# A graph layer whose table is multiplied first: W*W1 formed once, one product behind each pair of tiles, six banks for the sums

## The chip, the cores and the metric

One core of a Trainium2 chip. The metric is the device time of one execution in microseconds; the kernel before is given as the median of its runs, the kernel after will be.

## What is computed

Four residual layers over `x` of 6250 x 256 (float32), each behind a layer norm: a graph layer, a feed-forward layer of 8 experts, a second graph layer, a second expert layer. The change is in the second graph layer, cut here to what matters:

```python
row_sl = concatenate([row, sl]); col_sl = concatenate([col, sl])   # 100000 edges and 6250 self-loops
norm = dinv[row_sl] * ew_sl * dinv[col_sl]
xw = h6_all @ W                                                     # 256 x 256
msgs = xw[col_sl] * norm[:, None]
h7 = segment_sum(msgs, row_sl, num_segments=N) + b
h = relu(h7 @ W1 + b1)
out = h @ W2 + b2
```

The sum over edges is linear, so W may be applied to the rows ahead of the sum or to the sum behind it, and so may W1, since nothing stands between `+ b` and `@ W1`.

## The kernel before

The nodes are 49 tiles of 128 rows; a pair of tiles is the unit of the dense work behind the second aggregation (25 pairs, the last of one tile). `X` (the residual stream) stays in SBUF.

**Aggregation.** The edges, ordered by destination, are cut into 830 items of 128 edges, each item within one tile. For each item GpSimd gathers 128 table rows from DRAM (`aggregate_gpsimd`, L768) into a ring of twelve; it may start item i when the sum of item i-12 is made. DVE forms the one-hot matrix of the item's 128 destinations; PE multiplies one-hot by rows into a PSUM bank (`aggregate_tensor`, L757); DVE adds the bank to the tile's sums in SBUF (`add_sums`, L724). The first layer runs it over four banks with one-hots made eight at a time (L709, double-buffered). The second layer runs it over two banks (0 and 1), with one one-hot for each item that already carries the edge's weight (`one_hot`, L716, one instruction, four buffers). PE waits for the one-hot, the ring slot and the bank (the add of item i-2).

**Tables.** For the first layer each tile's rows are normed (ACT L1047, DVE), transposed by PE, copied by ACT (L1053), multiplied by W0 (PE L1079), copied by ACT (L1059) and stored. For the second layer (`second_table_scalar`, `norm_tiles_sync`) the rows are only normed: in seven groups of seven tiles, expert outputs are loaded (L1543), added to X by DVE (L1556), normed (ACT L586) and stored to the table (L595). Behind it come the item records (L675, transposed at L681, unpacked at L695 to L699) and the nine loads of the layer's weights on SyncE (L1595 to L1601); GpSimd, and the other engines of the aggregation, wait for these loads (`gw_in`, L1795).

**Heads.** When a pair's sums are complete, its dense work is done between the items, in eleven steps three items apart (`due`, `when_on_time`): 0 scale by degree (DVE L1666), 1 transposes (PE L1773, bank 2), 2 copy (DVE L1659), 3 product by W (PE L1722, eight matmuls, bank 3) and bias (ACT L1714), 4 product by W1 (L1722, bank 4) and relu (ACT L1705), 5 product by W2 (L1753, bank 5), 6 add to X and statistics (DVE L1650, L539), 7 norm (L564), 8 transposes (PE L1183, bank 6) and copy (ACT L1695), 9 gate product (PE L1734, bank 7), 10 logits and top two (DVE L1626 to L1634). If the ends of the tiles' edges lie too far from an even spread, `by_lateness` takes a second schedule (`when_late`); in the profile the even one runs.

**Around it.** `ffn0` ends with softmax over the gate's logits (`choose0`, exponential at L1370), then come the routing and the experts' products, then the second table. The second expert layer follows the last head (first instruction DVE L1824).

## Time and profile before

| | |
|---|---|
| median of 3 runs | 4323.81 us (4317.14 to 4326.35) |
| profiled execution | 4344.83 us, its span 4343.1 us, mean granted clock 0.82 |
| busy share of the span | PE 72%, DVE 58%, POOL 53%, ACT 23% |
| first aggregation, first gather to last add | about 146 to 1574 us |
| second aggregation | about 2505 to 3736 us |

PE is TensorE (PEld its weight loads), DVE VectorE, ACT ScalarE, POOL GpSimd, SP SyncE; a q behind a name is that engine's queue of DMA issues. Times in rows are microseconds from the start of the span; "[2.08 <-remote]" is idle time ahead of the instruction and what ended it, "issue" a time in which the profile shows nothing that it waited for, "remote" an event whose source the profile does not name. The granted clock of 1.00 is 2.4 GHz, 0.50 is 1.2 GHz.

### The profile page before, as it was taken

The numbers are of one execution on the slowest core, as the hardware profiler recorded it, in microseconds if no ns is written. First come the engines' busy times: TensorE is split into PE (matmuls) and PEld (weight loads), VectorE is DVE, ScalarE is ACT, GpSimd is POOL, SyncE is SP. The second block draws the span as 40 slices with busy tenths as digits, with TensorE's granted clock in tenths as the row PEclk, the third lists the DMA queues.
The fourth block names the chain that finished last, engine by engine and source line by source line (L and its number), as shares of the span: only waits on it lengthen the run. The fifth ranks groups of instructions, "written<-read, shape, count | busy, mean of one in ns | idle before, by whom it ended". The sixth has DMA issues, their size and how long they took to land.

```text
span 4343.1 us, 48949 instructions
## 1 busy us (share of the span) xinstructions
PE 3125.5 (72%) x13242; PEld 2272.2 (52%) x13242; DVE 2512.9 (58%) x6428; ACT 1020.2 (23%) x2553; POOL 2281.8 (53%) x2217
## 2 busy tenths in 40 slices
PE   4676766677777776778699256667666766688997
PEld 3454655566666653445588234444444444455555
DVE  5577888888777765443522545555555555642332
ACT  3443433444444332222111200000000000011221
POOL 1565655677777730000044166666666666477776
PEclk8776677889888987889799667777777787799999
DMA  4232222233333321112144433333333333623333
GB/s 135 84 90 73 82 62 67 76 83 84 82 82 83 83 75 58 73 58 83 41 151 150 154 90 99 103 99 101 100 100 99 105 101 98 146 44 54 54 53 45
DMA packets 188761, 380.01 MB, mean 87 GB/s; under 512 B 42140, under 2 KB 113192, under 8 KB 188105
## 3 DMA queue, kind: packets, MB, share of 16 engines
q0 software_dynamic: 121488, 285.06, 25.6%
q1 hardware_dynamic: 57964, 82.57, 5.4%
q10 hardware_dynamic: 9036, 9.15, 0.7%
q8 instruction: 123, 2.02, 0.2%
q14 instruction: 150, 1.22, 0.1%
HBM read 301.05 MB, written 77.44 MB: 87 GB/s over the span
## 4 chain that ended last, share of the span: by engine, by line
PE 44%; DVE 23%; issue 14%; POOL 6%; another core or an unknown queue 5%; DMA 3%; ACT 2%; DVEq 2%; SPq 0%; POOLq 0%; ACTq 0%
PE bank L757 16%; DVE acc_or_weights L724 7%; PE bank L1347 5%; PE bank L1532 4%; PE bank L1183 3%; PE bank L989 3%; POOL out_rows L1948 3%; PE bank L925 3%; PE bank L1722 2%; PE bank L1364 2%; POOL normed L1925 2%; DVE normed L909 1%; POOL normed L1929 1%; DVE acc_or_weights L869 1%
## 5 line engine op out<-in xcount | busy, mean ns | idle before, releaser
L768 POOL DMA_INDIRECT ring_or_weights<-gather_table,item_other_node x1660 | 1656.0, 998 | 990.7 <-issue 439.9
L724 DVE TENSOR_TENSOR acc_or_weights<-bank,acc_or_weights 128x257 f32 (+1 forms) x1660 | 703.9, 424 | 820.7 <-PE bank L757 413.1
L757 PE MATMUL bank<-ring_or_weights 128*128 128x256 f32 x1660 | 665.2, 522 | 398.7 <-DVE acc_or_weights L724 212.5
L757 PE MATMUL bank<-ring_or_weights,normed 128*128 128x257 f32 x1660 | 670.9, 496 | 91.2 <-DVE acc_or_weights L724 59.4
L757 PEld LDWEIGHTS bank<-ring_or_weights 128*128 128x128 f32 x1660 | 348.4, 245 | 673.1 <-issue 644.1
L989 PEld LDWEIGHTS bank<-normed,acc_or_weights 128*128 128x128 f32 x1564 | 346.8, 236 | 322.2 <-ACT acc_or_weights L980 172.1
L978 ACT ACTIVATE acc_or_weights<-iota_row,ring_or_weights 128x128 f32<-128x128 f32 x782 | 315.1, 403 | 702.2 <-PE bank L989 466.3
L989 PE MATMUL bank<-normed,acc_or_weights 128*128 128x49 f32 x1564 | 320.1, 292 | 176.6 <-ACT acc_or_weights L980 116.1
L1183 PE MATMUL bank<-identity,normed 128*128 128x128 f32 x1764 | 273.7, 287 | 230.3 <-DVE normed L564 167.0
L1483 POOL DMA_INDIRECT normed<-hidden_rows,item_weight x56 | 53.5, 956 | 621.6 <-DVE item_weight L1436 602.9
L757 PEld LDWEIGHTS bank<-ring_or_weights,normed 128*128 128x128 f32 x1660 | 320.5, 238 | 113.0 <-issue 107.0
L1183 PEld LDWEIGHTS bank<-identity,normed 128*128 128x128 f32 x1764 | 211.0, 146 | 322.1 <-DVE normed L564 129.9
L925 PE MATMUL bank<-normed 128*128 128x128 f32 x1564 | 263.1, 320 | 150.4 <-DVE normed L913 114.8
L925 PEld LDWEIGHTS bank<-normed 128*128 128x128 f32 x1564 | 225.5, 222 | 167.9 <-DVE normed L913 126.3
L716 DVE TENSOR_SCALAR ring_or_weights<-iota_row,item_local_node,item_weight 128x128 f32<-128x128 f32 x830 | 291.8, 352 | 3.4 <-issue 3.4
L980 ACT ACTIVATE acc_or_weights<-acc_or_weights 128x128 f32<-128x128 f32 x782 | 243.6, 312 | 24.9
L1347 PE MATMUL bank<-ring_or_weights,normed 128*128 128x512 f32 x392 | 234.4, 755 | 0.0
L1948 POOL DMA_INDIRECT out_rows<-normed,item_weight x105 | 170.3, 1622 | 83.3 <-issue 49.7
L1844 DVE TENSOR_TENSOR normed<-bank,ring_or_weights 128x512 f32<-128x512 f32 x105 | 72.6, 692 | 236.9 <-PE bank L1902 233.8
L1532 PE MATMUL bank<-acc_or_weights,normed 128*128 x896 | 203.2, 380 | 0.0
L1902 PE MATMUL bank<-acc_or_weights,normed 128*128 x420 | 200.9, 601 | 0.0
L1714 ACT ACTIVATE normed<-bank,bias_columns 128x256 f32<-128x256 f32 (+1 forms) x50 | 20.7, 465 | 765.5 <-PE bank L1722 430.3
(333 smaller groups left out, 4173.0 us busy)
## 6 DMA issues: line engine op xcount, KB each, us to landing
ring_or_weights<-gather_table,item_other_node POOLq DMA_INDIRECT x1660
hidden_rows<-normed SPq DMA_DIRECT2D x49, 512.0 KB
acc_or_weights<-in_L_ffn_Wd SPq DMA_DIRECT2D x8, 1024.0 KB, 5.4
acc_or_weights<-in_L_ffn_W SPq DMA_DIRECT2D x16, 512.0 KB, 9.9
gather_table<-normed SPq DMA_DIRECT2D x7, 896.0 KB, 4.1
gather_table<-acc_or_weights SPq DMA_DIRECT2D x7, 896.0 KB, 4.0
gather_table<-normed SPq DMA_DIRECT2D x24, 256.0 KB
out_rows<-x_rows SPq DMA_DIRECT2D x24, 256.0 KB
```

Source lines behind the costliest of these rows:

```text
L716: v.tensor_scalar(onehot[:, i % 4, :], iota[:, :], dloc[:, i:i + 1], wt[:, i:i + 1], ALU.is_equal, ALU.mult).then_inc(hot_made, 1)
L724: v.tensor_tensor(into, bank[i % nbank][:, 0:width], into, ALU.add).then_inc(added, 1)
L757: m.matmul(bank[i % nbank][:, 0:width], lhsT=hot, rhs=ring[:, i % RING, 0:width], start=True, stop=True).then_inc(sum_made, 1)
L768: g.indirect_dma_start(ring[:, i % RING, 0:D], None, table, IndirectOffsetOnAxis(ap=gidx[:, i:i + 1], axis=0)).then_inc(ring_in[i % RING], 16)
L925: last = m.matmul(group_bank(n)[:, 0:2 * LO], lhsT=row_hot[:, b % 2, c, :], rhs=spread[:, b % 2, c, :, :].rearrange("p k r -> p (k r)"), s ...
L978: s.activation(lo_tmp, iota[:, :], ACT.Abs, bias=neg_lo[:, i:i + 1]).then_inc(lo_abs, 1)
L980: s.activation(lo_hot[:, i % 2, :], lo_tmp, ACT.Relu, bias=1.0, scale=-1.0).then_inc(lo_done, 1)
L989: m.matmul(bank[7][:, 0:T], lhsT=lo_hot[:, j % 2, :], rhs=tile_hot[:, j // HOTS % 2, j % HOTS, :], start=j == 0, stop=j == EC - 1).then_in ...
L1183: last = m.transpose(to[:, k * P:(k + 1) * P], rows[:, k * P:(k + 1) * P], ident[:, :])
L1347: last = m.matmul(bank[2 + half][:, :], lhsT=xt[:, u % 2, k * P:(k + 1) * P], rhs=w1a[:, k, cols], start=k == 0, stop=k == KD - 1)
L1532: last = m.matmul(bank[4 + u % 2][:, 0:D], lhsT=ht[:, u % 2, c * P:(c + 1) * P], rhs=wd[:, ds(regs[u // 4][u % 4] + c * D, D)], start=c == ...
L1948: g.indirect_dma_start(out, IndirectOffsetOnAxis(ap=to_row[:, u:u + 1], axis=0), ys1[:, u % 4, :], None, bounds_check=N - 1, oob_is_err=Fa ...
```

## The change

1. The nine weight loads move from behind the item records to the beginning of `ffn0`'s SyncE work (`second_weights_sync`). Between `ffn0` and the softmax, PE transposes W (four transposes), multiplies by W1 (four matmuls), and forms the bias b*W1 + b1 (four small matmuls); ACT copies the results out (`both_weights_tensor`, `both_weights_scalar`).
2. The second table gets the first one's treatment: norm, transpose, copy, product by W*W1, copy, store (`norm_rows_scalar`, `norm_product_tensor`, `row_product_tensor`, shared by both layers now).
3. The second aggregation uses banks 0 to 5 for sums; all PSUM use of the heads shares banks 6 (`PING`) and 7 (`PONG`). One-hots are made eight at a time in two DVE instructions, compare and multiply by the weights, both over 128 x 1024.
4. Heads have nine steps: the copy, both products by W and W1 and the ACT bias are gone; ACT applies relu and bias straight to the transposed sums. The last pair is due 17 items later, so that the last two pairs no longer interleave on the two shared banks.

```diff
-    def one_hot(i):
-        if i >= 4:
-            v.wait_ge(sum_made, ITEMS + i - 3)
-        v.tensor_scalar(onehot[:, i % 4, :], iota[:, :], dloc[:, i:i + 1], wt[:, i:i + 1],
-                        ALU.is_equal, ALU.mult).then_inc(hot_made, 1)
+        hot = (hot1, hot2)[l][:, b % 2 * HOTS:b % 2 * HOTS + n, :]
+        equal = v.tensor_tensor(hot, iota[:, :].unsqueeze(1).broadcast_to([P, n, P]),
+                                dloc[:, cols].unsqueeze(2).broadcast_to([P, n, P]), ALU.is_equal)
+        if l == 0:
+            equal.then_inc(hots_in, 1)
+        else:
+            equal.then_inc(hots_in, 1)
+            v.wait_ge(hots_in, HOT_BATCHES + 2 * b + 1)
+            v.tensor_tensor(hot, hot, wt[:, cols].unsqueeze(2).broadcast_to([P, n, P]), ALU.mult).then_inc(hots_in, 1)
...
-            if l:
-                m.wait_ge(hot_made, i + 1)
-                hot = onehot[:, i % 4, :]
-            else:
-                m.wait_ge(hots_in, i // HOTS + 1)
-                hot = hot1[:, i % (2 * HOTS), :]
+            m.wait_ge(hots_in, HOT_BATCHES + 2 * (i // HOTS) + 2 if l else i // HOTS + 1)
+            hot = (hot1, hot2)[l][:, i % (2 * HOTS), :]
...
+    def norm_product_tensor(k, frm, n):
+        a = n * G7
+        for t in range(a, a + G7):
...
+            transpose_rows(frm[:, t, 0:D], bank[t % 2]).then_inc(rows_turned, 1)
+            if t >= 1:
+                row_product_tensor(k, t - 1)
...
+    def row_product_tensor(k, u):
+        m.wait_ge(turned_copied, k * T + u + 1)
+        if u >= 2:
+            m.wait_ge(prod_out, k * T + u - 1)
+        for c in range(KD):
+            last = m.matmul(bank[2 + u % 2][:, 0:D], lhsT=(row_t, row_t2)[k][:, u % 2, c * P:(c + 1) * P],
+                            rhs=(w0, w_both)[k][:, c, :], start=c == 0, stop=c == KD - 1)
+        last.then_inc(prod_made, 1)
...
+    def both_weights_tensor():
+        m.wait_ge(gw_in, GW)
...
+    def both_weights_scalar():
+        s.wait_ge(both_turned, 1)
+        s.activation(w_turned.rearrange("p k n -> p (k n)"), bank[0][:, :], ACT.Copy).then_inc(both_turned_out, 1)
+        s.wait_ge(both_made, 1)
+        for q in range(KD):
+            s.activation(b_both[:, q:q + 1], bank[4][:, q:q + 1], ACT.Identity, bias=bcol[:, 2 + q:3 + q])
+        s.activation(w_both.rearrange("p k n -> p (k n)"), bank[1][:, :], ACT.Copy).then_inc(both_out, 1)
...
     def ffn0_sync():
         load_expert0(E0 - 1)
+        second_weights_sync()
...
     def when_on_time(gi, n):
-        return PER_TILE * min(T, G2 * (gi + 1)) + MARGIN + 1 + STEP * n
+        return PER_TILE * G2 * (gi + 1) + MARGIN + 1 + STEP * n
...
+    SUM_BANKS, PING, PONG = 6, bank[6], bank[7]
...
-        aggregate_vector(1, D, 2, beside)
+        aggregate_vector(1, D, SUM_BANKS, beside)
...
-            for gi in due(when, 2, i):
-                a, n = pairs[gi]
-                v.wait_ge(a_tr, gi + 1)
-                if gi >= 2:
-                    v.wait_ge(b_mm, gi - 1)
-                v.tensor_copy(at_b[gi % 2][:, :, 0:n * P],
-                              bank[2][:, :].rearrange("p (k n) -> p k n", k=KD)[:, :, 0:n * P]).then_inc(a_in, 1)
...
+                    last = s.activation(ct_b[gi % 2][:, c, 0:n * P], PING[:, c * G2 * P:c * G2 * P + n * P],
+                                        ACT.Relu, bias=b_both[:, c:c + 1])
...
-            for gi in due(when, 4, i):
-                m.wait_ge(b_in, gi + 1)
-                if gi >= 1:
-                    m.wait_ge(c_in, gi)
-                product(bank[4], gcn_w[1], bt_b[gi % 2], pairs[gi][1]).then_inc(c_mm, 1)
-            for gi in due(when, 3, i):
-                m.wait_ge(a_in, gi + 1)
-                if gi >= 1:
-                    m.wait_ge(b_in, gi)
-                product(bank[3], gcn_w[0], at_b[gi % 2], pairs[gi][1]).then_inc(b_mm, 1)
```

## Rows read from the trace of the kernel before

**Rows 1.** Stretches: window, us, busy us (count) by engine, granted clock, DMA, GB/s

```profile
2422.00:2505.00 83.00, 3.64 (x15) 2.94 (x15) 51.97 (x196) 23.73 (x51) 0.00 (x1) 0.50 0.56 178
2505.00:3736.00 1231.00, 837.06 (x2584) 528.81 (x2584) 673.30 (x2149) 56.96 (x138) 788.08 (x830) 0.76 0.36 99
```

**Rows 2.** Groups of instructions from 2505 to 3736: busy us, mean ns, idle, releasers

```profile
L768 POOL DMA_INDIRECT ring_or_weights<-gather_table,item_other_node x830 | 788.1, 949 | 514.6 <-issue 255.1 <-PE bank L757 177.9 <-remote 81.6
L757 PE MATMUL bank<-ring_or_weights 128*128 128x256 f32 x1660 | 665.2, 522 | 398.7 <-DVE acc_or_weights L724 212.5 <-issue 170.5 <-DMA ring_or_weights<-gather_table,item_other_node 8.9
L724 DVE TENSOR_TENSOR acc_or_weights<-bank,acc_or_weights 128x256 f32 x830 | 352.1, 424 | 552.9 <-PE bank L757 306.7 <-remote 180.4 <-issue 49.4
...
L716 DVE TENSOR_SCALAR ring_or_weights<-iota_row,item_local_node,item_weight 128x128 f32<-128x128 f32 x830 | 291.8, 352 | 3.4 <-issue 3.4
L1722 PE MATMUL bank<-normed,edge_records_by_src 128*128 128x256 f32 x368 | 110.4, 454 | 0.0
```

**Rows 3.** Chain of waits from 2505 to 3725, shares by line

```profile
by line: PE bank L757 38.7%; issue 16.6%; another core or an unknown queue 11.1%; DVE acc_or_weights L724 10.7%; PE bank L1722 7.9%; PE bank L1753 3.0%; DVE ring_or_weights L716 2.3%; DVEq L96 1.5%; DVEq L724 1.1%; PE bank L1734 0.8%; PE ba
```

**Rows 4.** Timeline around 3127: start, us, what, [idle before <-releaser]

```profile
3125.33 0.94 POOL L768 DMA_INDIRECT ring_or_weights<-gather_table,item_other_node  x1 [0.30 <-issue]
3126.58 0.95 POOL L768 DMA_INDIRECT ring_or_weights<-gather_table,item_other_node  x1 [0.30 <-issue]
3129.47 0.43 DVE L724 TENSOR_TENSOR acc_or_weights<-bank,acc_or_weights 128x256 f32 x1 [5.12 <-remote]
3129.60 0.94 POOL L768 DMA_INDIRECT ring_or_weights<-gather_table,item_other_node  x1 [2.08 <-remote]
```

**Rows 5.** Groups of instructions from 146 to 1574 (first layer's aggregation)

```profile
L768 POOL DMA_INDIRECT ring_or_weights<-gather_table,item_other_node x830 | 867.9, 1046 | 476.1 <-PE bank L757 219.1 <-issue 184.8 <-remote 43.1
...
L913 DVE TENSOR_TENSOR normed<-normed,edge_records_by_src 128x512 f32<-128x512 f32 x196 | 135.6, 692 | 6.7
...
L709 DVE TENSOR_TENSOR normed<-iota_row,item_local_node 128x1024 f32<-128x1024 f32 x104 | 126.2, 1214 | 0.0
```

**Rows 6.** Timeline of the first layer around 302, DVE and POOL

```profile
302.32 1.21 DVE L709 TENSOR_TENSOR normed<-iota_row,item_local_node 128x1024 f32<-128x1024 f32 x1
302.43 1.92 POOL L768 DMA_INDIRECT ring_or_weights<-gather_table,item_other_node  x1 [0.30 <-issue]
```

**Rows 7.** Timeline of ACT in the first table's products

```profile
43.06 3.04 ACT L1047 ACTIVATE normed<-x_rows,norm_shift,rstd 128x256 f32<-128x256 f32 x6
...
48.53 0.38 ACT L1059 ACTIVATE normed<-bank 128x256 f32<-128x256 f32 x1 [1.64 <-PE bank L1079]
...
50.57 0.38 ACT L1059 ACTIVATE normed<-bank 128x256 f32<-128x256 f32 x1 [1.23 <-PE bank L1079]
...
55.30 3.04 ACT L1047 ACTIVATE normed<-x_rows,norm_shift,rstd 128x256 f32<-128x256 f32 x6
...
65.65 3.04 ACT L1047 ACTIVATE normed<-x_rows,norm_shift,rstd 128x256 f32<-128x256 f32 x6
```

**Rows 8.** Timeline of the second table and the start of its gathers

```profile
2441.90 3.06 ACT L586 ACTIVATE acc_or_weights<-x_rows,norm_shift,rstd 128x256 f32<-128x256 f32 x6 [0.30 <-DVE norm_shift L560]
...
2486.52 2.55 ACT L586 ACTIVATE acc_or_weights<-x_rows,norm_shift,rstd 128x256 f32<-128x256 f32 x5
...
2496.15 0.43 SPq L1601 DMA_DIRECT2D edge_records_by_src<-in_L_ffn_bias  x1
...
2505.00 0.98 POOL L768 DMA_INDIRECT ring_or_weights<-gather_table,item_other_node  x1 [85.51 <-issue]
```

**Rows 9.** Timeline at the end of the first feed-forward layer

```profile
2117.56 0.53 ACT L1370 ACTIVATE item_local_node<-item_local_node 128x392 f32<-128x392 f32 x1 [3.71 <-DVE item_local_node L1374]
```

**Rows 10.** Timeline of the last pairs' heads

```profile
3721.23 0.94 POOL L768 DMA_INDIRECT ring_or_weights<-gather_table,item_other_node  x1 [0.30 <-issue]
...
3736.20 0.69 DVE L1659 COPY normed<-bank 128x512 f32<-128x512 f32 x1
...
3757.77 0.24 DVE L1824 TENSOR_TENSOR token_gate<-normed 128x49 f32<-128x49 f32 x1
```

262 lines of the change are left out of this document (126 added, 136 removed).

## The prediction

> **What bounds the kernel now.** I read the table of stretches first: the second aggregation takes 1231 us of the span, and no engine is full in it: POOL works 788 us of it, PE 837, DVE 673, at a mean granted clock of 0.76 [rows 1]. So I went to the groups of instructions and to what ended their idle time. A gather costs 949 ns and starts 1.25 us after the last when nothing holds it (3125.33 to 3126.58, idle 0.30 "issue") [rows 2, 4]. 830 of them at 1.25 us are 1038 us; the stage needs 1216 us from the first gather (2505.00) to the last (3721.23) [rows 8, 10]. The 178 us between are the stage's loss, and POOL's own idle time gives the same figure: 177.9 us of it end with PE's sum L757 [rows 2]. POOL waits there for the sum of twelve items ago. Why is that sum late? PE waits 212.5 us for DVE's adds and DVE waits 306.7 us for PE's sums [rows 2]: with two banks each can be only two items ahead of the other, and neither can make good a delay. The chain agrees: 38.7% L757, 10.7% L724, 7.9% the products L1722, of both kinds 57% [rows 3]. A second source stands beside it: 11.1% of the chain is "an unknown queue", seen in the timeline as a sum whose data are there but whose end is reported late, so that the add starts after 5.12 us of idle time and the gather after 2.08 [rows 3, 4]. I don't know its cause; it is a risk below.
>
> **The change, part by part.** The sum is made against the profiled execution: span 4343.1, 1.7 us around it, 4344.8 in all. That is 21 us above the median of 4323.8; I carry the difference over to the median unchanged.
>
> *W\*W1 and its bias, once.* ACT's exponential at 2117.56 ends 3.71 us of idle time and waits only for DVE's L1374 [rows 9]; PE is idle there too. The new work begins when PE has made the last logits, so beside the few DVE steps ahead of the exponential. In series: four transposes, half as wide as L1722's matmuls, at up to 0.3 each; four matmuls at 0.45 [rows 2], four of one column; between and behind them four ACT instructions, of which a 256-wide norm is 0.51 (3.06 by six) [rows 8]: about 1 + 2 + 0.5 + 2, near 6 us. I take +5 for what shows, bounds +3 and +8 (low clock). The nine loads moved to `ffn0` lie on SyncE's queue ahead of the layer's other loads and stores there; hidden by 540 us of computing, 0, at most +3.
>
> *Second table.* Now ACT norms six tiles of seven in 3.06 us and the groups come at the pace of loads and DVE; the first starts at 2441.90, the last ends at 2486.52 + 2.55 = 2489.07 [rows 8]. After, each group is norm plus seven times transpose, copy, product, copy, on banks 0 to 3, ACT's two copies of a tile waiting alternately for PE. The first layer has exactly this: 12.24 us for a group begun cold (43.06 to 55.30), 10.35 for the next (55.30 to 65.65) [rows 7]. Seven groups from 2441.90: 2514.4 at 10.35, 2527.6 at 12.24. PE has done nothing before (clock 0.50 in this stretch, 3.64 us busy) [rows 1]; if it stayed at 1.2 GHz, a tile would cost the 2.04 us between 48.53 and 50.57 [rows 7], a group 3.04 + 7x2.04 = 17.3, the end 2563. I take the middle of the first two, 2521, since the first layer climbs within a group: +32 against 2489. Behind it stand 15.9 us to the first gather (2505.00) now, part of which is the weights' loads, issued until 2496.15 + 0.43 with GpSimd waiting for their landing [rows 8]; this goes, worth 0 to 2.5, I take 2. Net **+30**, bounds +23 and +74. ACT also issues half of the loads of expert outputs; they queue behind its copies now, but three buffers are ahead, so I price it at nothing; if they were late they would cost inside the same bounds.
>
> *Six banks.* PE may run six items ahead of DVE. A hold of 2 to 5 us [rows 4] then costs the gathers nothing as long as the ring of twelve (15 us of gathers) isn't exhausted and PE and DVE are faster than 1.25 us an item between holds. Are they? DVE's work falls from 673.3 us: minus L716 (291.8), plus 208 batch instructions at 1214 ns (252.5) [rows 1, 2, 5], minus the 23 copies (16): 618 us, 0.74 an item. PE: 837 minus the products' 110.4 [rows 1, 2] = 727, 0.88 an item. Both are under 1.25, with room to make good a hold. So POOL becomes the bound, and its loss of 178 us goes, at most.
>
> *Batched one-hots.* Here the change gives back. A DVE instruction with two SBUF inputs lengthens gathers: in the first layer's aggregation, where L709, L909 and L913 run, a gather takes 1046 ns against 949 [rows 2, 5], and beside one L709 a gather takes 1.92 us [rows 6]. Over 830 gathers that is 80 us, for 104 L709 and some 400 shorter ones; shared by single cases in the timeline, L709 takes about 0.30 us each, the others 0.15 or less. L716 reads its second and third operand as a value per partition and leaves the gathers at 949. After, 104 batches have two such instructions back to back: 208x0.30 = **62 us**. Bounds: 0 (they fall between gathers), and 1.4 us a batch, 146 us (a gather starts at each instruction's beginning, 0.97 for the first as in [rows 6], the rest for the second).
>
> The Trainium skill ("SBUF — State Buffer", section "SBUF: two separate sides") says that a DVE instruction with two SBUF inputs and a GpSimd one that reads SBUF hold the shared port pair in turn, each for its whole length. The trace agrees that such pairs lengthen gathers, 1.92 us beside L709, but not to that size on average: L709 and L913 alone are busy 262 us in the first layer, the gathers grew by 80 [rows 5]. What the rule would give here is the third rival.
>
> Stage: 1216 - 178 + 62 + 10 for holds that the ring doesn't absorb = 1110, 1.34 us an item, **-106**, bounds -178 and -22.
>
> *Heads.* Nine steps, 368 matmuls fewer, inside the stage and already in the sum of PE. At the end, from the last gather (3721.23) to the next layer's first instruction (3757.77) are 36.5 us [rows 10]. The first head instruction behind the last sums stands at 3736.20, 15 us behind the last gather [rows 10], because twelve items are still queued; with PE close behind the gathers it comes some 10 us sooner. Of the dense chain behind, the copy (0.69), sixteen matmuls (7.3 at 0.45 each, less where the clock is high) and two ACT instructions go, 5 to 8 us for a pair; but the last two pairs now follow one another on PING and PONG instead of overlapping, which gives most of that back. **-14**, bounds -18 and 0.
>
> Sum: +5 + 30 - 106 - 14 = **-85**: 4344.8 - 85 = 4260 for such an execution, 4323.8 - 85 = 4239 for the median.
>
> **Rivals.**
> *Full gain.* The batch instructions cost gathers nothing: -62 more, and the 10 us too: 4239 - 72 = 4167. For it: gathers run at 1.25 whenever not held. Against it: the 97 ns more in the first layer, which has the same instruction.
> *Late reports stay, at low clock.* The unexplained late ends of sums aren't caused by the two banks. PE's 0.88 an item is at clock 0.76; at 1.2 GHz it is 0.88x0.76/0.50 = 1.33, no faster than the gathers, and then holds aren't made good. If half of the 178 us stays (89, of which 10 are in my sum), the time is 4239 + 79 = 4318, no change that counts; if a quarter (45), 4274. For it: the holds have clock changes about them, and PE's "issue" idle time is 170.5 us [rows 2]. Against it: with more banks PE is idle less and the first layer, with four, has fewer of them.
> *The batch blocks the gathers (slower).* Each of the two instructions keeps POOL from its next gather for its whole 1.21 us: 2.43 a batch, 252 us in all. The stage becomes 1038 + 252 = 1290, +74; with +35 before it and -14 behind, +95: 4419. It decides the sign from 1.5 us a batch: the gains are 178 + 14, the other costs 35, so 157 us over 104 batches. A gather next to one L709 has paid 0.97 us [rows 6], two of them would be 1.9; the mean of the first layer, 0.30, speaks against it.
> *Second table at 1.2 GHz.* +74 instead of +30: 4283; not slower by itself.
> *The banks weren't the bound.* If POOL's waits were for something that six banks don't touch, only the costs remain, 4323.8 + 35 + 62 = 4420. Against it: the waits of PE for L724 and of DVE for L757 are the two largest after POOL's own [rows 2]; I leave it 3 in 100.
>
> **How the numbers follow.** Forecast, 4200 to 4275: 48 in 100. Full gain or near it, below 4200: 12. Late reports or a slow table, partly, 4275 to 4315: 22; within 0.2% of before, which is about what a measurement of this kernel can tell from no change (4315 to 4332): 6. Slower: batch blocks 9, banks not the bound 3. Time 4239. The range leaves out the slower cases and some 4 in 100 on each side of it: 4172 to 4322. Faster by over 0.2%: 0.82; within: 0.06; slower: 0.12.
>
> **What would show it.** The first gather about 30 us later than 2505; the groups of the second table 10 to 12 us apart on ACT. In the aggregation POOL busy about 850 us for 830 gathers, mean near 1025 ns; its idle time on L757 gone from 178 us to under 30, and PE's on L724 nearly gone; the chain there led by POOL, not by L757. L709's two forms at 1.21 us each. The last add within 5 us of the last gather's landing. What would make it wrong: a mean gather over 1.12 us (the port), holds of 3 to 5 us on PE that keep the ring full (late reports), a granted clock near 0.5 in the second table or in the aggregation, or a new wait of PE for `hots_in` because DVE makes a batch too late.

## The result, and the profile after

| | before | changed |
|---|---|---|
| median | 4322.88 us, 4 runs (4317.14 to 4326.35) | 4362.55 us, 4 runs (4358.94 to 4366.81) |
| ratio | | 1.0093, 95% interval 1.0076 to 1.0111 |
| profiled execution | 4344.8 us, span 4343.1 | 4358.9 us, span 4357.2 |

The change makes the kernel 40 us slower; 85 us faster was forecast. The two profiled executions differ by 14 us only, since that of before lay 22 us above its median and that of the changed kernel 4 us below its own. "Last layer" below is all that follows the first instruction of the second expert layer, "the stage" the time from the second aggregation's first gather to its last.

The second aggregation in the trace of the changed kernel, first its stretch (columns as in [rows 1]), then its chain of waits (as [rows 3]), then the groups that answer to [rows 2]; L802 is the gather, L791 the sum's matmul, L768 the add, L754 and L761 the two instructions of a batch:

```profile
2551.00:3760.00 1209.00, 745.36 (x2213) 485.69 (x2214) 692.09 (x1504) 37.72 (x92) 830.07 (x830) 0.72 0.36 101
```

```profile
by line: PE bank L791 21.4%; another core or an unknown queue 19.9%; issue 19.7%; DVE acc_or_weights L768 14.7%; DVE normed L754 6.1%; POOL ring_or_weights L802 2.5%; DVEq L96 2.2%; PE bank L1767 1.8%; DVEq L768 1.4%; DMA ring_or_weights<-g
```

```profile
L802 POOL DMA_INDIRECT ring_or_weights<-gather_table,item_other_node x830 | 830.1, 1000 | 501.5 <-issue 210.0 <-DVE item_other_node L740 131.1 <-remote 88.0
L791 PE MATMUL bank<-ring_or_weights,normed 128*128 128x256 f32 x1660 | 632.3, 520 | 373.4 <-DVE acc_or_weights L768 181.7 <-issue 168.2 <-DVE normed L761 18.1
...
L768 DVE TENSOR_TENSOR acc_or_weights<-bank,acc_or_weights 128x256 f32 x830 | 351.5, 423 | 505.6 <-remote 219.8 <-PE bank L791 149.2 <-issue 71.4
L761 DVE TENSOR_TENSOR normed<-normed,item_weight 128x1024 f32<-128x1024 f32 x104 | 127.2, 1223 | 3.5
L754 DVE TENSOR_TENSOR normed<-iota_row,item_local_node 128x1024 f32<-128x1024 f32 x104 | 126.4, 1215 | 3.2 <-issue 3.2
```

What to see: the waits of the engines for each other shrank, but less than forecast. DVE's idle time that ends with L791 fell from 307 us to 149, POOL's from 178 to 72 (under 30 was forecast), and L757's 38.7% of the chain became 21.4%. But PE still waits 182 us for adds with six banks, which can only be if DVE is six items behind; and DVE's idle time that ends with "remote" rose from 180 to 220 us, the unknown queue's share from 11.1% to 19.9%. A gather takes 1000 ns instead of 949, 42 us in all. The stage, first to last gather, fell from 1216.2 to 1199.5 us, by 17 and not by 106.

Such remote waits in the trace of the changed kernel, as a timeline:

```profile
2889.78 1.19 PE L791 MATMUL bank<-ring_or_weights,normed 128*128 128x256 f32 x2 [0.50 <-issue]
...
2891.68 2.90 PE L791 MATMUL bank<-ring_or_weights,normed 128*128 128x256 f32 x6
...
2896.56 0.42 DVE L768 TENSOR_TENSOR acc_or_weights<-bank,acc_or_weights 128x256 f32 x1 [4.18 <-remote]
...
2901.46 0.43 DVE L768 TENSOR_TENSOR acc_or_weights<-bank,acc_or_weights 128x256 f32 x1 [2.08 <-remote]
...
2903.57 0.43 DVE L768 TENSOR_TENSOR acc_or_weights<-bank,acc_or_weights 128x256 f32 x1 [1.68 <-remote]
...
2906.28 1.88 PE L1750 MATMUL bank<-edge_records_by_src,normed 128*128 128x8 f32 x8 [11.71 <-issue]
2906.46 0.42 DVE L768 TENSOR_TENSOR acc_or_weights<-bank,acc_or_weights 128x256 f32 x1 [2.46 <-remote]
```

PE has recorded its matmuls six items ahead of the adds by 2894.6, and four adds then wait one after another, 1.7 to 4.2 us each, for sums whose matmuls stand in the trace as ended. Before, with two banks, PE can be no more than two sums ahead [rows 4]. I call this late ends: the trace shows when the sum's semaphore rose, here microseconds behind the recorded matmul, and not what PE did between.

The table, in the changed kernel, ACT's and DVE's rows at some of the seven groups (L596 the norms of a group, L608 the last copy, L1581 the load of expert outputs, L1594 its use; for [rows 8]):

```profile
2442.39 3.06 ACT L596 ACTIVATE acc_or_weights<-x_rows,norm_shift,rstd 128x256 f32<-128x256 f32 x6 [0.29 <-DVE norm_shift L565]
...
2467.09 0.37 ACTq L1581 DMA_DIRECT2D normed<-expert_out  x1
...
2467.62 3.04 ACT L596 ACTIVATE acc_or_weights<-x_rows,norm_shift,rstd 128x256 f32<-128x256 f32 x6
...
2479.13 2.86 DVE L1594 SCALAR_TENSOR_TENSOR x_rows<-normed,token_gate,x_rows 128x256 f32<-128x256 f32 x7 [22.39 <-DMA normed<-expert_out]
...
2485.19 0.21 ACT L557 ACTIVATE rstd<-rstd 128x7 f32<-128x7 f32 x1 [5.57 <-DVE rstd L551]
2485.70 3.06 ACT L596 ACTIVATE acc_or_weights<-x_rows,norm_shift,rstd 128x256 f32<-128x256 f32 x6 [0.30 <-DVE norm_shift L565]
...
2507.32 2.86 DVE L1594 SCALAR_TENSOR_TENSOR x_rows<-normed,token_gate,x_rows 128x256 f32<-128x256 f32 x7 [14.56 <-DMA normed<-expert_out]
...
2513.38 0.21 ACT L557 ACTIVATE rstd<-rstd 128x7 f32<-128x7 f32 x1 [5.21 <-DVE rstd L551]
...
2537.99 0.38 ACT L608 ACTIVATE acc_or_weights<-bank 128x256 f32<-128x256 f32 x1 [0.48 <-PE bank L628]
...
2551.15 0.98 POOL L802 DMA_INDIRECT ring_or_weights<-gather_table,item_other_node  x1 [131.11 <-DVE item_other_node L740]
```

In the trace of before, the same ACT queue's load was issued 18.4 us earlier, and DVE waited 3.57 us for the loads and not 22.39:

```profile
2448.68 0.37 ACTq L1543 DMA_DIRECT2D normed<-expert_out  x1
...
2459.29 2.86 DVE L1556 SCALAR_TENSOR_TENSOR x_rows<-normed,token_gate,x_rows 128x256 f32<-128x256 f32 x7 [3.57 <-DMA normed<-expert_out]
```

And W*W1 ahead of the softmax, and the end (for [rows 9, 10]; L1339 the last logits, L1283 the product W*W1, L1408 the exponential and the load of its table, L1828 the first instruction of the next layer):

```profile
2107.99 0.17 DVE L1339 TENSOR_TENSOR item_local_node<-bank,normed 128x8 f32<-128x8 f32 x1 [1.99 <-PE bank L1402]
...
2109.58 3.78 PE L1283 MATMUL bank<-edge_records_by_src,normed 128*128 128x256 f32 x8 [0.69 <-ACT normed L1294]
...
2115.40 1.28 ACT L1408 ACT_TABLE_LOAD   x1
2116.70 0.53 ACT L1408 ACTIVATE item_local_node<-item_local_node 128x392 f32<-128x392 f32 x1
...
3750.70 0.95 POOL L802 DMA_INDIRECT ring_or_weights<-gather_table,item_other_node  x1 [0.30 <-issue]
...
3760.21 0.42 DVE L768 TENSOR_TENSOR acc_or_weights<-bank,acc_or_weights 128x256 f32 x1 [1.03 <-PE bank L791]
...
3782.07 0.25 DVE L1828 TENSOR_TENSOR token_gate<-normed 128x49 f32<-128x49 f32 x1
```

In the trace of before, ACT's table load stood ahead of the last logits (L1301):

```profile
2112.57 1.28 ACT L1370 ACT_TABLE_LOAD   x1
...
2116.15 0.17 DVE L1301 TENSOR_TENSOR item_local_node<-bank,normed 128x8 f32<-128x8 f32 x1 [1.91 <-PE bank L1364]
```

### The profile page after: what moved, and what is told of

The parts are those of the page before. It is cut to its first block, busy times and chain, and to the rows that moved or that the text cites. A ratio compares the mean times of both kernels' runs of the same rounds, so it can differ in the third digit from the quotient of the medians.

```text
span 4357.2 us, 48205 instructions
## 1 busy us (share of the span) xinstructions
PE 3091.0 (71%) x13156; PEld 2278.3 (52%) x13156; DVE 2527.4 (58%) x5781; ACT 1033.3 (24%) x2605; POOL 2327.0 (53%) x2217
## 4 chain that ended last, share of the span: by engine, by line
PE 36%; DVE 27%; issue 15%; another core or an unknown queue 8%; POOL 7%; ACT 3%; DMA 2%; DVEq 2%; POOLq 0%; ACTq 0%; SPq 0%
PE bank L791 11%; DVE acc_or_weights L768 8%; PE bank L1385 5%; PE bank L1570 4%; PE bank L1180 3%; POOL out_rows L1952 3%; PE bank L959 3%; DVE normed L754 3%; PE bank L1023 3%; PE bank L1402 2%; POOL normed L1929 2%; DVE normed L943 1%; POOL normed L1933 1%; PE bank L628 1%
## 5 line engine op out<-in xcount | busy, mean ns | idle before, releaser
L802 POOL DMA_INDIRECT ring_or_weights<-gather_table,item_other_node x1660 | 1703.8, 1026 | 967.0 <-issue 397.7
L791 PE MATMUL bank<-ring_or_weights,normed 128*128 128x257 f32 (+1 forms) x3320 | 1292.4, 504 | 467.8 <-DVE acc_or_weights L768 245.0
L768 DVE TENSOR_TENSOR acc_or_weights<-bank,acc_or_weights 128x257 f32 (+1 forms) x1660 | 703.3, 424 | 770.0 <-remote 290.1
L791 PEld LDWEIGHTS bank<-ring_or_weights,normed 128*128 128x128 f32 x3320 | 697.6, 245 | 707.1 <-issue 571.4
L754 DVE TENSOR_TENSOR normed<-iota_row,item_local_node 128x1024 f32<-128x1024 f32 x208 | 252.6, 1214 | 3.2 <-issue 3.2
L1570 PE MATMUL bank<-acc_or_weights,normed 128*128 x896 | 204.5, 382 | 0.0
L1914 PE MATMUL bank<-acc_or_weights,normed 128*128 x840 | 198.6, 379 | 1.8 <-ACT normed L1880 1.8
L1906 PE MATMUL bank<-acc_or_weights,normed 128*128 x420 | 199.3, 597 | 0.0
L1914 PEld LDWEIGHTS bank<-acc_or_weights,normed 128*128 128x128 f32 x840 | 159.4, 190 | 68.4 <-issue 52.1
L1329 DVE TENSOR_TENSOR normed<-bank,normed 128x512 f32<-128x512 f32 x98 | 67.8, 692 | 219.6 <-PE bank L1385 219.6
```

Of the source, the lines that this page charges most:

```text
L754: equal = v.tensor_tensor(hot, iota[:, :].unsqueeze(1).broadcast_to([P, n, P]), dloc[:, cols].unsqueeze(2).broadcast_to([P, n, P]), ALU.is ...
L768: v.tensor_tensor(into, bank[i % nbank][:, 0:width], into, ALU.add).then_inc(added, 1)
L791: m.matmul(bank[i % nbank][:, 0:width], lhsT=hot, rhs=ring[:, i % RING, 0:width], start=True, stop=True).then_inc(sum_made, 1)
L802: g.indirect_dma_start(ring[:, i % RING, 0:D], None, table, IndirectOffsetOnAxis(ap=gidx[:, i:i + 1], axis=0)).then_inc(ring_in[i % RING], 16)
L1570: last = m.matmul(bank[4 + u % 2][:, 0:D], lhsT=ht[:, u % 2, c * P:(c + 1) * P], rhs=wd[:, ds(regs[u // 4][u % 4] + c * D, D)], start=c == ...
L1914: last = m.matmul(bank[5 + u % 2][:, 0:D], lhsT=h1t[:, u % 2, c * P:(c + 1) * P], rhs=w2e[:, ds(regs[u // 4][u % 4] + c * D, D)], start=c ...
```

## The experiments

"Before" is timed beside each set. The sets came in two kinds, though nothing in the kernel differs: in some before took 4087 to 4089 us, in the others 4309 to 4313, about as in the first comparison (4323). I call them the sets of 4089 and of 4311. What makes the difference is open; the record gives the chip of each set by number, and 6 and 13 each have a set of either kind, so the number doesn't tell them apart. I compare medians within a set; where two traces of different sets are compared, they are of the same kind.

**First set (4089): four parts of the change.**

Single one-hots (the changed kernel; sixteen buffers, seven ahead):

```diff
-            if i % HOTS == 1 and (i // HOTS + 1) * HOTS < ITEMS:
+            if l and i + AHEAD < ITEMS:
+                one_hot(i + AHEAD)
+            if not l and i % HOTS == 1 and (i // HOTS + 1) * HOTS < ITEMS:
                 one_hots(l, i // HOTS + 1)
```

> The changed kernel, but each item's one-hot is made by one DVE instruction with two per-partition scalars again, seven items ahead of the add, in sixteen buffers, so that PE can still run six items ahead. Theory A (the batches' two-input instructions lengthen the gathers and fill DVE): the mean gather falls from 1000 to 950 ns, 42 us, and the batches' bursts go; about 4362 - 45 to 4362 - 70 = 4290 to 4317. Theory B (the late reports of PE's sums alone hold the stage): mean gather 950 ns, but the gained time turns into more waiting for sums, total within 15 us of 4362.

Two banks: `SUM_BANKS, PING, PONG = 2, bank[6], bank[7]`.

> The changed kernel with two sum banks instead of six, nothing else. Theory A (six banks help, the batches and the table ate it): slower than the changed kernel by 60 us or more, 4420 and above. Theory B (late reports, six banks change nothing): within 15 us of 4362. Rival C (running six ahead makes the late reports longer, 256 us of holds against 173): faster than 4362 by 10 to 60 us.

Both of these edits, with one-hots two ahead in four buffers:

> The changed kernel with the aggregation of before: two sum banks and one one-hot for each item, two ahead, four buffers. What is left of the change is W*W1, the product in the second table and the shorter heads. The table costs 46 us in the profile. Heads: 368 matmuls (110 us) less on PE. Theory A (two banks tie PE and DVE, PE's products on the chain, 7.9%): the heads give back up to 90 us, total 4323 + 46 + 5 - 90 = about 4285. Theory B (late reports bound the stage, products don't matter): 4323 + 46 + 5 = about 4374.

The table as before (W*W1 is formed but not applied, which is what it leaves out):

```diff
-            second_table_tensor()
...
-            y.wait_ge(prod_out, k * T + a + G7)
+            y.wait_ge(applied_v, k * GROUPS + n)
+            y.wait_ge(applied_s, (k * GROUPS + n) * (G7 - 1))
```

> The changed kernel without the transposes, copies and products in the second table: the rows are stored as normed (W*W1 isn't applied, which is the part left out). If the table's cost is the 46 us by which the first gather moved, 4362 - 46 = 4316, within 10 us; if part of it was hidden or the stage behind reacts, 4330 to 4350.

| | median | to before | stage, us | mean gather, ns |
|---|---|---|---|---|
| single one-hots, six banks | 4129.5 | 1.0097 (1.0081 to 1.0112) | 1042.6 | 951 |
| batches, two banks | 4178.3 | 1.0220 (1.0199 to 1.0241) | 1086.0 | 995 |
| single one-hots, two banks | 4137.4 | 1.0115 (1.0100 to 1.0131) | 1040.4 | 948 |
| changed, plain table | 4137.2 | 1.0108 (1.0092 to 1.0124) | 1093.0 | 1012 |

The expectations were written for 4323 and their absolute numbers fell with the set. What stays is the differences. With six banks or two the changed kernel takes the same (4180.0, measured in the next set, and 4178.3), as theory B has it, and what is left with single one-hots and two banks is before + 49 us, where theory B has 51. Theory A has the gathers right: they are back at 950 ns. Batches cost 41 us with two banks and, by the changed kernel's ratio in the next set, 49 with six; gathers longer by 47 and 66 ns, 830 of them, are 39 and 55 us of stage. The stage stands at 1040 to 1043 us whenever the one-hots are single, 1.255 to 1.258 us a gather.

**Second set (4089): the kernels themselves and two parts alone on the kernel before.**

> The changed kernel itself, timed and profiled beside the next ones. Its ratio to before was 1.0093 where before took 4323 us. In the last set before took 4088 us, the gathers of the second aggregation ran at their floor of 1.25 us and PE had no holds. Theory C (on a chip without holds six banks have nothing to give, and the batches lengthen the gathers by 50 us): ratio 1.02 to 1.025 where before takes 4088, 1.007 to 1.012 where before takes 4323. Theory D (the ratio doesn't depend on the holds): 1.009 in both.

> The kernel before, for its profile beside the others of this set. Theory C: where it takes 4088 us, the second aggregation has no late reports and takes 1038 to 1045 us from the first to the last gather, 830 gathers at 1.25 us; where it takes 4323, about 1216 us.

Six banks alone; heads on the two others, steps 0 to 10 as before (step 1 PING, W PONG, W1 PING, W2 PONG, transposes PING, gate PONG), one-hots single. The weights' loads and the last pair's place stay as the change has them, so "nothing else" below holds but for these two:

> The kernel before with one part of the change alone: six sum banks, its heads' PSUM use put on the two others (all eleven steps, both products), one-hots still one for each item but seven ahead in sixteen buffers so that PE can run ahead. Nothing else: no product in the table, no W*W1. Theory C: within 0.3% of before where before takes 4088 (gathers at their floor either way); where it takes 4323, faster by up to 178 us if the holds are covered by the run-ahead, or by less than 60 if late reports come in a row.

Batches alone:

> The kernel before with one-hots in batches of eight by two DVE instructions, two banks and everything else as before. Theory C: mean gather 995 to 1010 ns instead of 949, so +40 to +55 us on a chip where gathers run at their floor, 4128 to 4143 against 4088; where before takes 4323, part of it is hidden in waits, 0 to +40. Rival (batches are free next to gathers): within 10 us of before.

| | median | to before | stage, us | mean gather, ns |
|---|---|---|---|---|
| changed | 4180.0 | 1.0218 (1.0204 to 1.0232) | 1097.1 | 1017 |
| before | 4091.3 | 1.0003 (0.9993 to 1.0013) | 1042.6 | 951 |
| six banks alone | 4091.7 | 1.0007 (0.9998 to 1.0016) | 1041.9 | 950 |
| batches alone | 4148.5 | 1.0146 (1.0130 to 1.0161) | 1101.1 | 1004 |

Theory C held on each point but one: the batches alone cost 59 us, a little over the 40 to 55 expected. By the trace 44 us of it are the longer gathers (53 ns each), and some 14 are gathers that started late because POOL waited for PE's sum L748; with six banks (changed, second set) no gather started late for a sum. The groups of the kernel before in this set show why six banks have nothing to give here:

```profile
L768 POOL DMA_INDIRECT ring_or_weights<-gather_table,item_other_node x830 | 789.4, 951 | 340.3 <-issue 228.5 <-PE bank L757 111.8
L757 PE MATMUL bank<-ring_or_weights 128*128 128x256 f32 x1660 | 639.4, 495 | 260.1 <-DVE acc_or_weights L724 93.4 <-DMA ring_or_weights<-gather_table,item_other_node 70.5 <-issue 52.0
L724 DVE TENSOR_TENSOR acc_or_weights<-bank,acc_or_weights 128x256 f32 x830 | 351.5, 423 | 374.6 <-PE bank L757 358.7 <-issue 5.1 <-DVE x_rows L1675 2.5
```

No "remote" at all, and PE waits for landings: two banks already keep up with the gathers. In [rows 2] the same kernel has 81.6 us of remote waits on POOL and 180.4 on DVE. See also POOL's 111.8 us that end with L757: the gathers start at their floor here, and every one has 0.30 us of idle time ahead of it, which is put down to L757 where a sum came just then. Such idle time is no loss.

How a batch lengthens a gather, in the timeline of the batches alone in the second set (L759 the gather, L711 compare, L718 multiply):

```profile
2501.76 1.22 DVE L711 TENSOR_TENSOR normed<-iota_row,item_local_node 128x1024 f32<-128x1024 f32 x1
2501.81 1.98 POOL L759 DMA_INDIRECT ring_or_weights<-gather_table,item_other_node  x1 [0.30 <-PE bank L748]
2503.01 1.23 DVE L718 TENSOR_TENSOR normed<-normed,item_weight 128x1024 f32<-128x1024 f32 x1
2504.10 0.95 POOL L759 DMA_INDIRECT ring_or_weights<-gather_table,item_other_node  x1 [0.31 <-issue]
```

A gather that starts 0.05 us into L711 takes 1.98 us, 1.03 more than its 0.95. Those that start in the first 0.2 us of it take 0.82 more on average, at 0.4 to 0.6 us 0.59, at 0.8 to 1.0 us 0.20, after 1.1 us nothing. The held gather ends 0.8 us behind L711 wherever it began inside the first microsecond of it, and the next one starts 0.1 us ahead of L718's end: all 101 starts inside L718 lie after its first microsecond and aren't lengthened. So in this trace a batch holds one gather, whatever the second instruction. In the changed kernel's first trace, where gathers also wait for other reasons, two of the 95 that started inside the second instruction came early in it, at 0.25 and 0.68 us, and they took 1.53 and 1.36 us.

**Third set (4311): a version meant to be better, and the compare alone.** W*W1 formed once but applied behind the sums (table plain, eleven steps on two banks), six banks, single one-hots:

```diff
+            for gi in due(when, 3, i):
+                m.wait_ge(a_in, gi + 1)
+                if gi >= 1:
+                    m.wait_ge(g_in, gi)
+                product(PONG, w_both, at_b[gi % 2], pairs[gi][1]).then_inc(b_mm, 1)
```

> A version meant to keep what the change may give and drop what it costs: W*W1 formed once, but applied to the sums in one product behind each pair (the table is stored as normed, as before), one product and one ACT instruction fewer in the heads, eleven steps on two banks, six sum banks, one one-hot for each item seven ahead. Theory C: where before takes 4089 us the gathers are at their floor, so only +5 for W*W1 and a few us less at the last heads: 4085 to 4096. Where before takes 4323: the holds are partly covered, 4230 to 4300. Rival (the matmuls saved matter): 4060 or less on the first kind of chip.

> The same with two sum banks and one-hots two ahead in four buffers, as before. Theory C: within 5 us of the six-bank version where before takes 4089; where it takes 4323, slower than it by what six banks give there.

```diff
-            equal.then_inc(hots_in, 1)
-            v.wait_ge(hots_in, HOT_BATCHES + 2 * b + 1)
-            v.tensor_tensor(hot, hot, wt[:, cols].unsqueeze(2).broadcast_to([P, n, P]), ALU.mult).then_inc(hots_in, 1)
+            equal.then_inc(hots_in, 2)
```

> The changed kernel without the second instruction of each batch: the one-hots aren't multiplied by the edge weights, which is the part left out. In the traces so far a gather that starts inside the first instruction of a batch is held to its end (up to 1.05 us), and then the next gather falls at the very end of the second instruction, unheld. Theory E (only one gather of a batch can be held): the mean gather stays at 1000 to 1010 ns, time within 12 us of 4180. Rival (each two-input instruction costs 0.25 us): mean 975, 4155.

| | median | to before (4308.6) | stage, us | mean gather, ns |
|---|---|---|---|---|
| product behind, six banks | 4300.1 | 0.9976 (0.9965 to 0.9986) | 1188.4 | 949 |
| product behind, two banks | 4308.2 | 1.0003 (0.9992 to 1.0014) | 1196.7 | 953 |
| changed, compare only | 4341.9 | 1.0082 (1.0065 to 1.0098) | 1192.5 | 991 |

Compare only: the gather's mean fell by 9 ns against the 1000 of the changed kernel and its ratio is that of the changed kernel within the intervals (1.0082, 1.0093). It lies between the theories' 1000 to 1010 and 975, nearer to E. The product behind is 8 us faster with six banks than with two by the medians; six banks were expected to bring it to 4230 to 4300.

**Fourth and fifth set (4311): the late ends.** All heads behind the last item; PE draining its sum ahead of a block of head matmuls; the two parts alone again; sums of half the columns (the same width in the adds, `aggregate_vector`); single one-hots again:

```diff
-            ends = program(when_on_time)
+            ends = program(when_late)
```

> The kernel before with the heads of all pairs behind the last item (its second schedule) instead of between the items; nothing left out. Where before takes 4310 to 4323 us, 20 to 40 sums of the second aggregation end 3 to 5 us late, and they cluster at the items at which a pair's block of head matmuls is issued (item 15, 21, 27, 2 and 5 of a pair's 34). Theory F (the late ends belong to these blocks): without heads the stage runs at 1.25 to 1.27 us an item, 1040 to 1055 us from the first to the last gather, also there. Rival (late ends belong to the chip whatever PE does): 1150 us or more. The total is longer in both by the heads behind, some 25 times 10 to 18 us.

```diff
+            if l and (i - MARGIN - 1) % (2 * PER_TILE) in [STEP * n % (2 * PER_TILE) for n in (1, 3, 4, 5, 8, 9)]:
+                m.wait_ge(sum_made, l * ITEMS + i + 1)
             beside(i)
```

> The kernel before, but PE waits for the end of its own last sum before it issues a block of head matmuls (six blocks for each pair). Theory F1 (a sum is reported late because the block is queued behind it): the late ends go, the stage falls by 50 to 150 us where before takes 4310 to 4323, total 4170 to 4270. Rival F2 (the block itself or its neighbours are slow there, in whatever order): the same within 15 us, or slower by up to 20. Where before takes 4089: 0 to +10 us.

> Six banks alone again, in a set in which before may take 4310 to 4323 us. In the last set of that kind six banks were worth 8 us with the product behind (4300 against 4308). If that holds: 0.997 to 0.999 of before. If run-ahead covers the holds: 0.97 or less. Where before takes 4089: 1.000 to 1.0015 as measured.

> Batches alone again. Where before takes 4089 it was 1.0146. Where before takes 4310 to 4323, a part of the 50 us of lengthened gathers lies in the holds: 1.001 to 1.008.

```diff
-        aggregate_tensor(1, D, 2, heads)
+        aggregate_tensor(1, D // 2, 2, heads)
```

> The kernel before, but the second aggregation's matmuls and adds take only the first 128 of the 256 columns (the other half of each sum is left out); gathers, heads, one-hots and waits as before. Where before takes 4310 to 4323 us: Theory G (PE's own throughput, with pauses that the trace shows as late ends, bounds the stage at about 1.45 us an item): with half the columns the stage falls to 1040 to 1100 us, total 4180 to 4230. Rival H (each pause comes with a number of instructions or of items, whatever their width): 1170 us or more, total within 50 us of before. Where before takes 4089: 1040 us either way.

> The changed kernel with single one-hots again, in a set in which before may take 4310 to 4323 us. There the stage takes 1184 to 1222 us in all versions so far, so the batches' lengthened gathers (45 us) are partly hidden in it: 1.004 to 1.009 of before against 1.0093 for the changed kernel. Where before takes 4089 it was 1.0097.

| | median | to before (4310.9, the last two 4313.1) | stage, us |
|---|---|---|---|
| heads after | 4445.0 | 1.0310 (1.0286 to 1.0334) | 1184.3 |
| sum drained first | 4327.2 | 1.0044 (1.0029 to 1.0059) | 1219.2 |
| six banks alone | 4317.5 | 1.0017 (1.0004 to 1.0029) | 1203.9 |
| batches alone | 4336.2 | 1.0068 (1.0043 to 1.0092) | 1222.1 |
| half-width sums | 4309.0 | 0.9993 (0.9978 to 1.0007) | 1203.6 |
| changed, single one-hots | 4346.5 | 1.0075 (1.0056 to 1.0093) | 1192.1 |

Theory F falls: with no head matmul in the stage it takes 1184 us. The late ends, which in the trace of before had clustered at the heads' items (25 of 49 at two of a pair's 34), are spread, at most 4 at one item, and fewer: DVE has 32 remote waits over 2 us against 47, 103 us in all against 180. So a part of them may belong to the heads, and the run says less than it seems, since PE ran the stage at a mean granted clock of 0.60 (0.76 before) and DVE waited 414 us for PE's recorded sums instead of 307. Draining first makes it slower by 16 us; F1 falls. Theory G falls too: half the matmul's columns, PE 169 us less busy, and no time is gained (rival H); here too the clock was low (0.61), so a matmul's mean fell from 522 to 426 ns and not by half. Six banks alone, where the forecast put 178 us and the expectation 0.997 to 0.999, give nothing; the groups of that run (L818 the gather, L807 the sum, L778 the add):

```profile
L818 POOL DMA_INDIRECT ring_or_weights<-gather_table,item_other_node x830 | 789.8, 952 | 498.4 <-issue 199.1 <-remote 124.0 <-PE bank L807 91.9
L807 PE MATMUL bank<-ring_or_weights,normed 128*128 128x256 f32 x1657 | 540.2, 466 | 184.0 <-DVE acc_or_weights L778 95.2 <-issue 76.8 <-DVE normed L770 7.0
...
L778 DVE TENSOR_TENSOR acc_or_weights<-bank,acc_or_weights 128x256 f32 x826 | 350.2, 424 | 551.2 <-remote 275.3 <-PE bank L807 190.5 <-issue 68.6
```

Against [rows 2], POOL's waits on L757 went from 178 to 92 and its remote ones from 82 to 124; DVE's from 307 to 191 and from 180 to 275. The waiting changed its name: counting only what goes beyond the 0.30 us that every gather has, POOL lost 177 us in the trace of before and 162 here. The half-width sums keep both with two banks:

```profile
L757 PE MATMUL bank<-ring_or_weights 128*128 128x128 f32 x1640 | 495.8, 426 | 488.6 <-DVE acc_or_weights L724 322.4 <-issue 144.3 <-DMA ring_or_weights<-gather_table,item_other_node 9.8
...
L724 DVE TENSOR_TENSOR acc_or_weights<-bank,acc_or_weights 128x128 f32 x818 | 237.8, 291 | 637.7 <-remote 294.9 <-PE bank L757 271.5 <-issue 63.7
```

**Last run (before 4086.5): the better version again.**

> The version with W*W1 applied behind the sums, six banks and single one-hots again. Where before takes 4310 to 4323 it was 0.9976. Theory C: where before takes 4089 the gathers are at their floor and only W*W1's forming (+7) and the shorter end (a few us less) count: 0.999 to 1.002. Rival: the 0.9976 comes from the saved matmuls and holds on either kind, 0.996 to 0.999.

4093.6 us, 1.0014 (1.0004 to 1.0024), stage 1041.4. Theory C: without late ends it is no gain, and W*W1's forming would be a small loss (+7 in the trace; the time's interval allows 2 to 10).

## Why the prediction was wrong

**The step that failed** is "Six banks": "So POOL becomes the bound, and its loss of 178 us goes, at most", worth -178 (bounds of the stage -178 and -22). I read the mutual waits of PE and DVE as the cause of the loss. They were where it showed. Six banks alone changed the time by +0.07% (4089, not clear of zero) and +0.17% (4311); with the product behind the sums they gained 0.27% by the ratios (4311). Where there are no late ends, two banks already let the gathers run at 1.255 us; where there are, the stage takes 1184 to 1222 us in eleven kernels with two or six banks, single or batched one-hots, with and without heads, with whole or half sums. The profile had said it in the "unknown queue"; I gave the second source only 10 us in the sum. The stage fell by 17 us where the forecast had 106, and that is 89 of the 99 us by which the sum of the profiled executions was off (4260 forecast, 4359 measured); the rest is W*W1 and the table (+46 for +5 and +30, so 11), the heads (+9) and the last layer (-10).

The figure that seemed to confirm the reading was luck. "POOL's own idle time gives the same figure", 177.9 us that end with L757, holds the floor's 0.30 us in it, and the second set's 111.8 us without any loss show what that is worth. Counting only what goes beyond the floor, POOL's loss of 177 us in that trace ends with L757 for 100, with "remote" for 65 and with "issue" for 11.

The rival "late reports stay" came nearest in time (4318), but its reason (PE at 1.2 GHz can't make good a hold) is not shown. The changed kernel in the second set ran the stage at a granted clock of 0.70 without one late end, and in the first trace of before the clock in DVE's remote waits was 0.83, above the stage's 0.76. With six banks the waits became longer instead: DVE's remote waits over 2 us are 4.4 us on average with six banks alone and 5.4 with the product behind, against 3.6 before and 3.1 with the product behind two. The rival "the banks weren't the bound", 3 in 100, names what six banks alone then showed; its 4420 was too high, since the 42 us by which the gathers grew did not lengthen the stage. My argument against it, that the two waits are the largest, is the error in one line: two engines that wait for each other each have a large wait, and neither need be the cause.

**Point by point.**
- *W\*W1*: forecast +5. Last logits to exponential took 8.7 us; before, the exponential followed the last logits by 1.4. +7, inside the bounds, and partly by luck. Two things were missing in the working: a float32 matmul of the program stands as two records in the trace (830 sums are x1660), so the four matmuls at 0.45 were eight records, 3.78 us and not 2; and ACT's load of the exponential's table, 1.28 us, which before lay ahead of the last logits, now lies behind W*W1's copies.
- *Second table*: forecast +30, bounds +23 to +74. First gather 46 us later in the first comparison, W*W1 included, and 53 measured from the last add of the first aggregation (which ended 7 us earlier); 51 in the second set. So about +44 to +46 for the table. The last copy ended at 2538.4 and not at 2521. Of these 17 us the greater part is the term that I "priced at nothing": ACT's loads. The load issued at 2467.09 instead of 2448.68 let DVE wait 22.4 us, the next one 14.6, and ACT stood idle behind each (5.57 and 5.21). The groups on ACT were 10.4 to 13.3 us apart without that and 18 with it. The other 6 us are the pace: 12.2 us a group without the idle times, the upper end of my two readings and not their middle. The granted clock in the stretch was 0.79, so the rival of a table at 1.2 GHz did not come about. Shown by the trace; the plain table took 43 us off (4180.0 to 4137.2, in two sets of 4089), as it should.
- *Batches*: forecast +62, bounds 0 and 146. The gathers grew by 42 us in the first comparison and 55 in the second set; with batches alone the kernel is 59 us slower in one kind of set and 25 in the other, where a part lies in the late ends. Right in size for the gathers, and for the time in the sets of 4089. In the sets of 4311, for which the forecast was made, little of it came through: the changed kernel with single one-hots stood at 1.0075 against 1.0093, some 8 us, and the intervals overlap. The mechanism was half right: two instructions don't cost twice, the second is hardly ever hit. A batch costs 0.4 to 0.5 us, where I had two times 0.30. The rule of the Trainium skill's page "SBUF — State Buffer" ("SBUF: two separate sides"), that whichever of the two starts first has the shared port pair for its whole instruction and the other blocks, is borne out one way: a gather that starts inside L711 ends 0.8 us after it, wherever in its first microsecond the gather began. The other way it isn't: where a gather is running already, neither it (947 ns on average) nor DVE's instruction (1215 ns) is lengthened. My rival's 2.43 us a batch was wrong because the gather behind the held one starts only at the end of the second instruction.
- *PE and DVE have room*: right, though not by my figure for DVE. It was busy 692 us in the stage's window and not 618, 0.83 us an item: L716's records and the adds' overlap in the trace of before (their sum with the heads' is 790 us, the busy time 673), so taking off all of L716's 291.8 took off too much. PE's 745 stand against 727. In the sets of 4089 nothing but POOL bounds the stage with single one-hots, or with batches and six banks.
- *Heads*: forecast -14. From the last gather to the next layer 36.5 us before, 31.4 after; -7 in the second set (43.3, 36.3). The twelve queued items did come sooner, the last add ended 9.9 us behind the last gather instead of 14.9 (10 us sooner was forecast). From the last add to the next layer it is 21.9 us against 22.0: the shorter chain of a pair gave nothing there, and that the two last pairs in a row took it is argued, not shown.
- *The rest*: the last layer took 10 us less in the profiled execution after than in that of before (575 and 585), and equally long in the second set. It belongs to that one execution, not to the change.

The second set's account closes: +51 W*W1 and table, +54.5 the stage, -7 the end, 98.4 between the spans (4082.1 and 4180.5); the medians differ by 91.

**What stays open**: what the late ends are, and so what held the stage at 1216 us. They aren't there in the sets of 4089, in any of the nine kernels traced. In each of the eleven others DVE has 24 to 72 remote waits over 2 us in the stage, 3.1 to 5.5 us on average. Not shown as a cause: the number of banks, the head matmuls, their order with the sums, the width of the sum, the granted clock. The packets of the gathers take about the same time inside and outside of these waits (165 and 162 ns on average in the trace of before), and 4 of the stage's 67 packets of instruction fetches fall into them, which is less than their share of its time (180 of 1216 us).

One difference between the two kinds stands in the traces themselves. The eleven of the sets of 4311 and of the first comparison hold 23,809 to 25,959 semaphore events each, the nine of the sets of 4089 hold 49,007 to 49,817; where a kernel was traced in both kinds, before for one (24,613 and 49,701), its instructions are the same in number, 48,949; of the 830 events of the second aggregation's sums the former hold 575 to 679, the latter all. Two things follow. In the former, a wait whose event isn't recorded is put down to something else, "issue" for one, so the shares of "PE", "remote" and "issue" there, [rows 2] and [rows 3] among them, are rough. And whether the recording of events, or what delays it, itself holds the engines is a rival that no run here tests. What speaks for it is that 248 of the 261 us between the two traces of before lie in the two aggregations, where the fuller trace holds 2500 to 3300 events in 200 us; against it, the last layer has some 2350 and took 585 and 575 us, 10 apart. It remains unproven. Kernels that gather less, or pace PE, were not tried.

## What to carry to other kernels

When two engines wait for each other, ask whether either would still wait if the other were instant, and run the buffers' part alone before you pay for it elsewhere. Count what each queue also issues before you give its engine more work: a load that stands behind a group's copies is a late load. Before you take an engine's idle time as a loss, look at a trace in which nothing is lost: part of it is a floor. And count the events that a trace holds before you read who waited for whom. A DVE instruction with two SBUF inputs costs a gather beside it what is left of it when the gather starts, so many short ones with scalar operands can be cheaper than few long ones, whatever DVE's own sum says: here by 41 to 50 us where the gathers bound the stage, and hardly at all where the late ends did.

## What the runs showed of the hardware

- The same kernel took 4089 us in some sets and 4311 to 4323 in others, 5.4 to 5.7% apart, with the same instructions and a similar granted clock (0.845 and 0.82 in the two traces of before). The second aggregation alone makes 174 us of it (1042.6 against 1216.2), the first 74 (1343.2 against 1417.3).
- A gather that starts inside a 1.215 us two-input DVE instruction is lengthened by up to 1.05 us, one that is running already is not (947 ns), and the DVE instruction keeps its length.
- Six banks in place of two let PE record its sums six items ahead; alone they left the stage at 1041.9 us for 1042.6 (4089) and 1203.9 for 1216.2 (4311), the time at +0.07% and +0.17%.
- A float32 matmul of the program is two records in the trace: 830 sums are x1660.
